# The carry of a chunked state-space scan: one 256-column product from high and low parts in place of two 128-column products

## The chip, the cores and the metric

The kernel runs on one core of one Trainium2 chip. A core has five engines that run side by side, each through its own list in order, and wait for one another by semaphores: TensorE (PE, matrix products), VectorE (DVE), ScalarE (ACT), GpSimd (POOL) and SyncE (SP, which here issues every DMA). The metric is the device time of one execution in microseconds (us), the median of several.

## The reference, cut to what matters

```python
x = x + mamba(layernorm(x), ...)      # 2 sequences x 512 tokens x 512 features, 128 heads of 64 columns, 8 groups
x = x + dense(layernorm(x)) + lora    # at the end, small

# inside mamba, per head (B and C are shared by the 16 heads of a group), 4 chunks of 128 tokens:
A_cum  = cumsum(A_dt, axis=-1)                                   # within each chunk
Y_diag = einsum('bzlhn,bzshn,bhzls,bzshp->bzlhp', Cc, Bc, L, xch)  # inside a chunk
states = einsum('bzlhn,bhzl,bzlhp->bzhpn', Bc, exp(A_cum[..., -1:] - A_cum), xch)
prev   = einsum('bhzc,bchpn->bzhpn', decay_chunk, states_p)[:, :-1]  # the state that enters each chunk
Y_off  = einsum('bzlhn,bzhpn,bhzl->bzlhp', Cc, prev, exp(A_cum))   # the carry: what it adds to the chunk
y = (Y_diag + Y_off + hs * D) * silu(gate)     # then a norm per group and an output product
```

The carry is `Y_off`: chunk 0 has none, chunks 1, 2 and 3 get the state that entered them, times their C, times a growth `exp(A_cum)`.

## The kernel before, in words

The work is cut into 64 **units** of two heads (128 feature columns) with both sequences (`b` = 0 and 1) in each. Eight units in a row make a **group**, which has one B and one C. I number the units 0 to 63; `k` is that number and `j` the place in the group, 0 to 7. Every engine has a loop over the groups with a body over `j`, written out by hand, and no scheduler moves anything. Projections and the output product are made with float32r operands (`F32R`), a number being cut into a high and a low part and three products summed (high by high, high by low, low by high). ACT makes each high part by a copy, POOL or DVE each low part by a subtraction.

In unit `k` the engines do this, in this order:

- **PE**: two output products of the pair before (`later_outs`), the projection of `x` for the next unit, `states` (L828 to L836, which waits for POOL's `xdecay`), `diagonal` (L838 to L846, which waits for DVE's `scores` and for two of DVE's output sums), the projection of the next gate, `carry` (L849 to L857, which waits for DVE's `state`), and two more output products. In units 4 and 5 of a group the next group's B and C are projected too.
- **DVE**: `scores`, then `xdt` (`to_heads`, L1357, from `quads`, which come by DMA), output sums, `y_low`, in units 1 to 3 of a group three or fewer normed sums, the three taps of the convolution of the next unit, `carried_state` (L1296), the block transpose of the next unit (`turn_blocks`, L1342), `skip`, `carry_part` (L1309) and `add_carry` (L1321) of both sequences, two output sums.
- **ACT**: the high part and the square of the unit before, `tap0` of the next (L1094, which waits for the projection of `x`), two weight high parts (L1072), then the decay factors, the SiLUs and the exponentials.
- **POOL**: `xdecay` (L1550, L1553), a weight low part (L1529), the running sum of squares (L1537), the low part of the output weight (L1571), a second weight low part, and the gate product of both sequences (`gated`, L1543).
- **SP**: in this order, among others, a weight load that waits for POOL's second low part (L702), the store of the turned blocks (`store_blocks`, L724, which waits for DVE's `turn_blocks`), the load of `quads` (L730, when the store has landed), and the growth rows of the next unit (`load_grown`, L717).

So SP's store stands behind its weight load: the blocks go out when DVE has turned them **and** POOL has made its second low part.

The carry before. `states` gives `P` columns for the carry of chunk 1 and, in the columns from `LATER * P`, the state at the middle, that is, the state which enters chunk 2. DVE copies it twice: as it is, and times the decay of chunk 2 (`chunk_tab`, a small table that has its own DMAs). `carry` then makes three float32 products of 128 columns per sequence: copy 0 by C of chunk 2, what chunk 2 itself adds (`xdecay[:, b, 2]`) by `bc_across[:, b, 1]`, and copy 1 by C of chunk 3, the last two summed. DVE multiplies the 384 columns by the growth rows and adds them to `y`.

## Time and profile before

| | |
|---|---|
| three runs | 1586.59, 1589.17, 1592.49 us; median 1589.17 |
| the profiled execution | 1586.06 us, of which its span is 1584.3 us |
| granted TensorE clock | 0.995 of full speed |
| busy, share of the span | PE 98%, PEld 82%, DVE 80%, ACT 72%, POOL 50% |
| DMA | 225.24 MB, 142 GB/s in the mean |

A row of a timeline has the start in us from the span's start, the time from the first start to the last end, the engine, the line, what is written and read, and how many in a row; brackets at its end give the time that the engine had been idle and who ended that. An engine pipelines: the next instruction can start a little before the row above has ended. PE's records are pipelined still more, so that a product's price is the distance from its start to the next start, not its length. A float32 product of 128 columns leaves two records, a float32r product one.

### The profile page before, as it was taken

How to read it: one execution, taken by the hardware profiler on the slowest of the kernel's cores; microseconds unless marked ns; L12 is line 12 of the kernel's file. 1: busy time of each engine (PE TensorE's matmuls, PEld its weight loads, DVE VectorE, ACT ScalarE, POOL GpSimd, SP SyncE). 2: the span in 40 equal slices, each digit the busy share in tenths (PEclk: the TensorE clock that was granted, in tenths of full speed). 3: DMA queues.
4: the chain of work that ended last, by engine and by line, in shares of the span. 5: the costliest groups of instructions: out<-in, count | busy, mean ns of one | idle time of the engine just before them, and what ended most of it. 6: DMA issues, size and time to landing. Idle time of an engine off the chain costs nothing.

```text
span 1584.3 us, 25865 instructions
## 1 busy us (share of the span) xinstructions
PE 1545.5 (98%) x9144; PEld 1304.9 (82%) x9144; DVE 1272.5 (80%) x1532; ACT 1142.7 (72%) x2020; POOL 790.6 (50%) x599
## 2 busy tenths in 40 slices
PE   7989999999999999999999999999999999999988
PEld 5768888888888888888888888878888888888877
DVE  6677777887879787887778878898778977798767
ACT  5976768875777667777687767767678767777743
POOL 2154545554545555455455545556544654555540
PEclk9999999999999999999999999999999999999999
DMA  4534445444444444543444444444444435444411
GB/s 153 203 113 152 130 144 168 155 135 146 139 148 152 148 140 128 170 160 115 159 156 151 134 154 146 137 147 156 130 147 165 150 120 165 142 150 150 131 44 53
DMA packets 130112, 225.24 MB, mean 142 GB/s; under 512 B 27840, under 2 KB 74944, under 8 KB 129728
## 3 DMA queue, kind: packets, MB, share of 16 engines
q1 hardware_dynamic: 129984, 223.59, 44.1%
q8 instruction: 73, 1.20, 0.3%
q14 instruction: 55, 0.45, 0.1%
HBM read 186.30 MB, written 37.23 MB: 141 GB/s over the span
## 4 chain that ended last, share of the span: by engine, by line
PE 44%; POOL 17%; DMA 13%; issue 11%; DVE 9%; ACT 4%; SPq 3%; DVEq 0%; POOLq 0%; ACTq 0%
DMA blocks_dram<-quads 7%; DMA quads<-blocks_dram 5%; POOL xdecay L1553 5%; POOL w_low L1529 4%; PE g_bank L824 4%; POOL square_sum L1537 4%; PE g_bank L826 4%; PE g_bank L825 4%; PE d_bank L845 4%; PE x_bank L826 3%; PE x_bank L824 3%; PE x_bank L825 3%; DVE xdt L1357 3%; SPq L730 2%; POOL out_low L1571 2%
## 5 line engine op out<-in xcount | busy, mean ns | idle before, releaser
L1082 ACT ACTIVATE scores<-scores,tables 128x128 f32<-128x128 f32 x1024 | 311.9, 389 | 0.0
L1543 POOL TENSOR_TENSOR y<-y,gate 128x512 f32<-128x512 f32 x128 | 190.1, 1506 | 209.3 <-DVE y L1325 209.3
L1529 POOL TENSOR_TENSOR w_low<-raw,w_high 128x512 fp32r<-128x512 f32 x139 | 186.1, 1339 | 202.5 <-ACT w_high L1072 202.5
L1261 DVE SCALAR_TENSOR_TENSOR hs<-x_bank,cols,hs 128x1022 f32<-128x1022 f32 x189 | 241.6, 1278 | 49.7 <-ACT hs L1094 45.1
L824 PE MATMUL g_bank<-x_high,w_high 128*128 128x512 f32 x624 | 250.5, 401 | 0.0
L826 PE MATMUL g_bank<-x_high,w_low 128*128 128x512 f32 x624 | 243.3, 390 | 0.0
L825 PE MATMUL g_bank<-x_low,w_high 128*128 128x512 f32 x624 | 243.2, 390 | 0.0
L1094 ACT ACTIVATE hs<-x_bank,cols 128x1024 f32<-128x1024 f32 x63 | 75.8, 1203 | 229.5 <-PE x_bank L826 167.8
L1293 DVE TENSOR_TENSOR scores<-scores,bc 128x1024 f32<-128x1024 f32 x128 | 188.3, 1510 | 16.4 <-ACT scores L1087 16.4
L824 PE MATMUL x_bank<-x_high,w_high 128*128 128x512 f32 x504 | 196.6, 390 | 0.0
L826 PE MATMUL x_bank<-x_high,w_low 128*128 128x512 f32 x504 | 196.1, 389 | 0.0
L825 PE MATMUL x_bank<-x_low,w_high 128*128 128x512 f32 x504 | 196.1, 389 | 0.0
L1550 POOL TENSOR_TENSOR xdecay<-xdt,tables 128x256 f32<-128x256 f32 x64 | 41.9, 655 | 306.3 <-DVE xdt L1357 292.1
L1357 DVE TENSOR_TENSOR xdt<-quads,tables 128x512 f32<-128x512 f32 x120 | 77.5, 687 | 89.2 <-DMA quads<-blocks_dram 85.8
L824 PEld LDWEIGHTS g_bank<-x_high,w_high 128*128 128x128 f32 x624 | 117.0, 188 | 33.2 <-issue 10.8
L1553 POOL TENSOR_TENSOR xdecay<-xdt,tables 128x384 f32<-128x384 f32 x128 | 143.4, 1141 | 0.0
L1537 POOL TENSOR_TENSOR square_sum<-square_sum,gate 128x1024 f32<-128x1024 f32 x55 | 139.1, 2530 | 0.0
L826 PEld LDWEIGHTS g_bank<-x_high,w_low 128*128 128x128 f32 x624 | 117.1, 188 | 25.4
L825 PEld LDWEIGHTS g_bank<-x_low,w_high 128*128 128x128 f32 x624 | 117.2, 188 | 22.4
L845 PE MATMUL d_bank<-scores,xdt 128*64 128x128 f32 x2048 | 126.6, 276 | 3.1 <-DVE acc L1380 2.2
L1087 ACT ACTIVATE scores<-scores 128x1024 f32<-128x1024 f32 x128 | 128.6, 1052 | 0.7
L845 PEld LDWEIGHTS d_bank<-scores,xdt 128*64 128x64 f32 x2048 | 111.0, 137 | 11.7 <-DVE acc L1380 3.4
(227 smaller groups left out, 3573.4 us busy)
## 6 DMA issues: line engine op xcount, KB each, us to landing
scores<-sums_dram SPq DMA_DIRECT2D x128, 512.0 KB, 5.0
raw<-w_in SPq DMA_DIRECT2D x144, 256.0 KB, 2.8
blocks_dram<-quads SPq DMA_DIRECT2D x60, 512.0 KB, 3.7
quads<-blocks_dram SPq DMA_DIRECT2D x240, 128.0 KB, 2.9
grown_rows<-grown_dram SPq DMA_DIRECT2D x256, 96.0 KB, 2.8
out_raw<-w_out SPq DMA_DIRECT2D x64, 256.0 KB, 3.0
mixed<-x SPq DMA_DIRECT2D x8, 256.0 KB, 4.9
out<-mixed SPq DMA_DIRECT2D x8, 256.0 KB, 2.0
```

The costliest lines, as they stand in the source:

```text
L824: pe.matmul(to, w_high[:, slot, k], x_high[:, b, k], start=(k == 0), stop=False)
L825: pe.matmul(to, w_high[:, slot, k], x_low[:, b, k], start=False, stop=False)
L826: mm = pe.matmul(to, w_low[:, slot, k], x_high[:, b, k], start=False, stop=(k == KT - 1))
L845: mm = pe.matmul(d_bank[r * HEAD_DIM:(r + 1) * HEAD_DIM, b, c * P:(c + 1) * P], xdt[:, b, c, r], scores[:, s, b, r, c], start=True, stop=True)
L1082: op = s.activation(at, at, ACT.Relu, bias=col[:, r, c:c + 1], scale=-1.0)
L1087: s.activation(scores[:, q % 2, b], scores[:, q % 2, b], ACT.Exp, scale=-1.0).then_inc(exp_ready, 1)
L1261: v.scalar_tensor_tensor(out=hs[:, q % 2, :, i:], in0=x_bank[:, :, 0:SEQ - i], scalar=cols[:, q, TAPS - 1 - i:TAPS - i], in1=hs[:, q % 2, ...
L1293: v.tensor_tensor(at, at, bc[:, b].rearrange("p c l -> p (c l)").unsqueeze(1) .to_broadcast([P, PAIR, SEQ]), ALU.mult).then_inc(scores_rea ...
L1529: pool.tensor_tensor(w_low[:, slot], raw[:, slot], w_high[:, slot].bitcast(F32), ALU.subtract)\
L1537: pool.tensor_tensor(square_sum[:], square_sum[:], gate[:, q % 2], ALU.add).then_inc(square_added, 1)
L1543: pool.tensor_tensor(y[:, b], y[:, b], gate[:, q % 2, b], ALU.mult).then_inc(y_ready, 1)
L1553: pool.tensor_tensor(xdecay[:, b, 0:LATER], xdt[:, b, 0:LATER], col.unsqueeze(3).to_broadcast([P, LATER, PAIR, HEAD_DIM]), ALU.mult)\
```

## The change

Chunks 2 and 3 lie side by side, so the state at the middle is multiplied by C of both at once, 256 columns, as three float32r products; what chunk 2 itself adds to chunk 3 becomes a product of its own into the first 128 columns. For this, the growth of chunk 3 is counted from the middle (the rows of chunk 3 get the sum at the end of chunk 2 as a bias), and chunk 3's own growth, for the separate product, takes the place of chunk 0's, which nobody used. In the loops:

- PE: `carry` is three float32r products of 256 columns and one float32 product of 128 columns for each sequence, in place of three float32 products of 128. It waits for `c_low_ready` in unit 0 of a group.
- DVE: `carried_state` writes a high part and then, after it, a low part, in place of two independent copies. `carry_part` covers 512 columns in place of 384.
- POOL: `gated` first adds 128 columns (the separate product) to chunk 3 of `y`, waits for that, and then multiplies by the gate. In unit 0 of each group POOL also makes `c_low`, 128x512, between its first weight low part and the sum of squares.
- SP: `load_grown` loads 512 columns a row in place of 384 and waits for POOL's new sum (`last_added`) in place of DVE's `y_sum`. The table `chunk_dram`, its stores, its loads and their waits are gone.
- ACT, before the loops: three exponentials for the growth (128, 256 and 128 columns) in place of one of 512; the copy for the chunk table is gone. `keep_c` writes a float32r tile of the same size.

```diff
@@ sync, prologue
-                sp.wait_ge(chunk_ready, b + 1)
-                sp.dma_start(chunk_by_head[b], chunk_decay[:, b]).then_inc(chunks_stored[b], 16)
...
@@ growth (ACT, prologue)
-                s.activation(grown[:, b], sums[:, b], ACT.Exp).then_inc(grown_ready, 1)
+                last = slice(LATER * P, (LATER + 1) * P)
+                s.activation(grown[:, b, 0:P], sums[:, b, last], ACT.Exp)
+                s.activation(grown[:, b, P:LATER * P], sums[:, b, P:LATER * P], ACT.Exp)
+                s.activation(grown[:, b, last], sums[:, b, last], ACT.Exp, bias=sums[:, b, last.start - 1:last.start])\
+                 .then_inc(grown_ready, 1)
...
-                s.activation(chunk_decay[:, b], grown[:, b, P - 1::P], ACT.Copy).then_inc(chunk_ready, 1)
@@ load_grown (SP)
-                reached(sp, y_sum, BATCH * (k - 1) + b + 1)
+                reached(sp, last_added, BATCH * (k - 1) + b + 1)
...
-                                 rows[r, P:].partition_broadcast(HEAD_DIM)).then_inc(grown_in[b], 16)
+                                 rows[r].partition_broadcast(HEAD_DIM)).then_inc(grown_in[b], 16)
@@ load_tables (SP)
-                reached(sp, state_ready, used)
-                load_chunks(g, b, half)
@@ states (PE)
-                pe.matmul(to[:, LATER * P:], b_tok[:, b, 0], part[:, 3], start=True, stop=False)
-                pe.matmul(to[:, LATER * P:], b_tok[:, b, 1], part[:, 1], start=False, stop=True)
-                pe.matmul(to[:, 0:P], part[:, 0], bc_across[:, b, 0], start=True, stop=True).then_inc(states_added, 1)
+                pe.matmul(to[:, 0:P], b_tok[:, b, 0], part[:, 3], start=True, stop=False)
+                pe.matmul(to[:, 0:P], b_tok[:, b, 1], part[:, 1], start=False, stop=True)
+                pe.matmul(to[:, P:2 * P], part[:, 0], bc_across[:, b, 0], start=True, stop=True).then_inc(states_added, 1)
@@ carry (PE)
-                pe.matmul(to[:, P:2 * P], state[:, b, 0].rearrange("p r d -> p (r d)"), c_feat[:, b, 0:P],
-                          start=True, stop=True)
-                pe.matmul(to[:, 2 * P:3 * P], xdecay[:, b, 2].rearrange("p r d -> p (r d)"), bc_across[:, b, 1],
-                          start=True, stop=False)
-                pe.matmul(to[:, 2 * P:3 * P], state[:, b, 1].rearrange("p r d -> p (r d)"), c_feat[:, b, P:],
-                          start=False, stop=True).then_inc(carried, 1)
+                pe.matmul(to[:, 2 * P:], state_high[:, b], c_high[:, b], start=True, stop=False)
+                pe.matmul(to[:, 2 * P:], state_high[:, b], c_low[:, b], start=False, stop=False)
+                pe.matmul(to[:, 2 * P:], state_low[:, b], c_high[:, b], start=False, stop=True)
+                pe.matmul(to[:, 0:P], xdecay[:, b, 2].rearrange("p r d -> p (r d)"), bc_across[:, b, 1],
+                          start=True, stop=True).then_inc(carried, 1)
@@ carried_state (DVE)
-                v.tensor_copy(state[:, :, 0], added_up).then_inc(state_ready, 1)
-                lost = chunk_tab[:, :, PAIR * q:PAIR * (q + 1), 2]
-                v.tensor_tensor(state[:, :, 1], added_up, lost.unsqueeze(3).to_broadcast([P, BATCH, PAIR, HEAD_DIM]),
-                                ALU.mult).then_inc(state_ready, 1)
+                v.tensor_copy(state_high[:], added_up).then_inc(state_ready, 1)
+                v.wait_ge(state_ready, 2 * k + 1)
+                v.tensor_tensor(state_low[:], added_up, state_high[:].bitcast(F32), ALU.subtract)\
+                 .then_inc(state_ready, 1)
@@ carry_part, add_carry (DVE)
-                v.tensor_tensor(rows, head_bank[b][:, 0:LATER * P], rows, ALU.mult).then_inc(carry_scaled, 1)
+                v.tensor_tensor(rows, head_bank[b], rows, ALU.mult).then_inc(carry_scaled, 1)
...
-                v.tensor_tensor(y[:, b, P:], y[:, b, P:], grown[:, b].rearrange("p c l -> p (c l)"), ALU.add)\
+                v.tensor_tensor(y[:, b, P:], y[:, b, P:], grown[:, b, 1:].rearrange("p c l -> p (c l)"), ALU.add)\
@@ gated (POOL)
                 pool.wait_ge(y_sum, u + 1)
+                pool.tensor_tensor(y[:, b, LATER * P:], y[:, b, LATER * P:], grown[:, b, 0], ALU.add)\
+                    .then_inc(last_added, 1)
+                pool.wait_ge(last_added, u + 1)
@@ body (POOL)
+                    if j == 0:
+                        pool.wait_ge(c_ready, g + 1)
+                        pool.tensor_tensor(c_low[:], bc_conv[:, 1, :, 2 * P:], c_high[:].bitcast(F32), ALU.subtract)\
+                            .then_inc(c_low_ready, 1)
```

On PE the place is the carry of one unit, between the gate projection and the output products; `c_feat`, `c_high` and `c_low` are C, `state*` the state at the middle, `group_parts` B and C put together. Before:

```order
L852 MATMUL head_bank<-c_feat,state 128x128
L854 MATMUL head_bank<-group_parts,xdecay 128x128
L856 MATMUL head_bank<-c_feat,state 128x128
L852 MATMUL head_bank<-c_feat,state 128x128
L854 MATMUL head_bank<-group_parts,xdecay 128x128
L856 MATMUL head_bank<-c_feat,state 128x128
```

Of the changed kernel, the same place:

```order
L839 MATMUL head_bank<-c_high,state_high 128x256
L840 MATMUL head_bank<-c_low,state_high 128x256
L841 MATMUL head_bank<-c_high,state_low 128x256
L842 MATMUL head_bank<-group_parts,xdecay 128x128
L839 MATMUL head_bank<-c_high,state_high 128x256
L840 MATMUL head_bank<-c_low,state_high 128x256
L841 MATMUL head_bank<-c_high,state_low 128x256
L842 MATMUL head_bank<-group_parts,xdecay 128x128
```

Six float32 products became six float32r products of twice the columns and two float32 ones; nothing else moved on PE.

On POOL the place is unit 0 of a group, from `xdecay` to the gate products. Before:

```order
L1553 TENSOR_TENSOR xdecay<-xdt,tables 128x384 x2
L1529 TENSOR_TENSOR w_low<-raw,w_high 128x512
L1537 TENSOR_TENSOR square_sum<-square_sum,gate 128x1024
L1571 TENSOR_TENSOR out_low<-out_raw,out_high 128x512
L1529 TENSOR_TENSOR w_low<-raw,w_high 128x512
L1543 TENSOR_TENSOR y<-y,gate 128x512 x2
```

Of the changed kernel, the same place:

```order
L1541 TENSOR_TENSOR xdecay<-xdt,tables 128x384 x2
L1514 TENSOR_TENSOR w_low<-raw,w_high 128x512
L1558 TENSOR_TENSOR c_low<-bc_conv,c_high 128x512
L1522 TENSOR_TENSOR square_sum<-square_sum,gate 128x1024
L1563 TENSOR_TENSOR out_low<-out_raw,out_high 128x512
L1514 TENSOR_TENSOR w_low<-raw,w_high 128x512
L1527 TENSOR_TENSOR y<-y,grown_rows 128x128
L1531 TENSOR_TENSOR y<-y,gate 128x512
L1527 TENSOR_TENSOR y<-y,grown_rows 128x128
L1531 TENSOR_TENSOR y<-y,gate 128x512
```

`c_low` now stands ahead of the second weight low part, in unit 0 of each group alone; the two sums of 128 columns stand ahead of the gate products in every unit.

## Rows read from the trace of the kernel before

**Rows 1.** The page: each engine's busy time, its share of the span, its instructions.

```profile
PE 1545.5 (98%) x9144; PEld 1304.9 (82%) x9144; DVE 1272.5 (80%) x1532; ACT 1142.7 (72%) x2020; POOL 790.6 (50%) x599
```

**Rows 2.** Waits: engine, line, for whom; us in total, times, longest.

```profile
PE head_bank L834 <- POOL xdecay L1553: 12.7, 8, 3.3
```

**Rows 3.** Timeline of PE in unit 32, from the gate projection into the carry.

```profile
823.25 0.39 PE L826 MATMUL g_bank<-x_high,w_low 128*128 128x512 f32 x1
823.48 0.38 PE L852 MATMUL head_bank<-c_feat,state 128*128 128x128 f32 x2
823.70 0.39 PE L854 MATMUL head_bank<-group_parts,xdecay 128*128 128x128 f32 x2
```

**Rows 4.** Timelines of POOL, DVE and SP in unit 32, by start.

```profile
816.58 1.29 POOL L1529 TENSOR_TENSOR w_low<-raw,w_high 128x512 fp32r<-128x512 f32 x1 [2.43 <-ACT w_high L1072]
821.44 1.30 POOL L1529 TENSOR_TENSOR w_low<-raw,w_high 128x512 fp32r<-128x512 f32 x1
821.77 1.25 DVE L1342 STREAM_TRANSPOSE quads<-hs 128x1024 f32<-128x1024 f32 x1 [1.18 <-ACT hs L1106]
822.77 0.33 SPq L702 DMA_DIRECT2D raw<-w_in  x1
823.27 0.32 SPq L724 DMA_DIRECT2D blocks_dram<-quads  x1
831.53 1.29 DVE L1357 TENSOR_TENSOR xdt<-quads,tables 128x512 f32<-128x512 f32 x2 [0.39 <-DMA quads<-blocks_dram]
```

**Rows 5.** Timelines of DVE and SP in units 33 and 35, by start.

```profile
843.81 1.25 DVE L1342 STREAM_TRANSPOSE quads<-hs 128x1024 f32<-128x1024 f32 x1 [0.77 <-ACT hs L1106]
845.09 0.32 SPq L724 DMA_DIRECT2D blocks_dram<-quads  x1
...
886.21 1.25 DVE L1342 STREAM_TRANSPOSE quads<-hs 128x1024 f32<-128x1024 f32 x1 [0.46 <-ACT hs L1106]
887.82 0.32 SPq L724 DMA_DIRECT2D blocks_dram<-quads  x1
```

**Rows 6.** Timelines of POOL and PE: `xdecay` and `states` of units 33 and 36.

```profile
833.48 2.63 POOL L1553 TENSOR_TENSOR xdecay<-xdt,tables 128x384 f32<-128x384 f32 x2
837.29 0.39 PE L834 MATMUL head_bank<-xdecay,group_parts 128*128 128x128 f32 x2
...
898.28 2.62 POOL L1553 TENSOR_TENSOR xdecay<-xdt,tables 128x384 f32<-128x384 f32 x2
900.95 0.49 PE L834 MATMUL head_bank<-xdecay,group_parts 128*128 128x128 f32 x2
```

**Rows 7.** Timelines of DVE and PE: output sums and `diagonal` of unit 38.

```profile
954.48 1.28 DVE L1380 TENSOR_TENSOR acc<-d_bank,acc 128x512 f32<-128x512 f32 x2
955.21 1.86 PE L845 MATMUL d_bank<-scores,xdt 128*64 128x128 f32 x30 [0.17 <-DVE acc L1380]
```

**Rows 8.** Groups of DVE by line and shape: busy us, mean ns, idle before.

```profile
L1313 DVE TENSOR_TENSOR grown_rows<-head_bank,grown_rows 128x384 f32<-128x384 f32 x128 | 70.1, 555 | 23.7 <-PE head_bank L856 16.6
L1380 DVE TENSOR_TENSOR acc<-x_bank,acc 128x512 f32<-128x512 f32 x96 | 64.9, 686 | 19.7 <-PE x_bank L894 19.5
```

**Rows 9.** Timelines of ACT and POOL behind the gate products of unit 35.

```profile
893.27 1.16 ACT L1130 ACTIVATE y_high<-y,cols 128x1024 fp32r<-128x1024 f32 x1 [0.47 <-POOL y L1543]
897.70 0.62 POOL L1550 TENSOR_TENSOR xdecay<-xdt,tables 128x256 f32<-128x256 f32 x1 [4.46 <-DVE xdt L1357]
900.24 1.21 ACT L1094 ACTIVATE hs<-x_bank,cols 128x1024 f32<-128x1024 f32 x1 [4.34 <-PE x_bank L826]
```

**Rows 10.** Timeline of DVE: `scores` of units 35 and 39.

```profile
871.54 2.78 DVE L1293 TENSOR_TENSOR scores<-scores,bc 128x1024 f32<-128x1024 f32 x2
969.47 2.36 DVE L1293 TENSOR_TENSOR scores<-scores,bc 128x1024 f32<-128x1024 f32 x2 [1.14 <-ACT scores L1087]
```

**Rows 11.** Timeline of ACT at the start: exponentials of the prologue, and the end of unit 0.

```profile
40.60 0.97 ACT L434 ACTIVATE one_plus<-head_sums 128x128 f32<-128x128 f32 x3
...
85.15 1.16 ACT L1130 ACTIVATE y_high<-y,cols 128x1024 fp32r<-128x1024 f32 x1 [1.97 <-POOL y L1543]
```

56 lines of the change are left out of this document (22 added, 34 removed).

## The prediction

> **What bounds the kernel now.** I read the page first: PE is busy for 98% of the span, DVE for 80, ACT for 72, POOL for 50 [rows 1]. So a saving on PE should count, if PE is never kept waiting. Then the waits: PE waited for POOL's `xdecay` 12.7 us in all, in 8 waits over the threshold of the view [rows 2]. That is little, but it shows a second path almost as long as PE's. I followed it through one group, units 32 to 39, on the timelines of all engines.
>
> It starts when the projection of `x` ends. ACT makes `tap0` and two weight high parts, POOL the first weight low part at 816.58 and the second from 821.44 to 822.74; SP's weight load has waited for this, goes at 822.77, and the store of the blocks behind it at 823.27. DVE had turned the blocks at 821.77 + 1.25 = 823.02 [rows 4]. So in unit 32 POOL is last by a quarter of a microsecond. `xdt` of unit 33 starts at 831.53, that is 8.26 us after the store. In unit 33 DVE is last (turned at 845.06, stored at 845.09), in unit 35 POOL's side again (886.21 + 1.25 = 887.46, stored at 887.82, 0.36 later) [rows 5]; unit 34 looks like unit 32, POOL last by 0.25.
>
> How long this path is against PE's is seen at `states`. In unit 33 the second sequence's `xdecay` is ready at 836.11 and PE takes it at 837.29: 1.18 us to spare. In unit 36 it is ready at 900.90 and PE takes it at 900.95: PE waits [rows 6]. The spare time melts by about 0.4 us a unit from unit 1 to unit 4 of a group, since DVE's normed sums make its round longer than PE's; units 5 and 6, in which PE projects B and C too, bring it back. The seven whole groups after the first all look like this: in unit 4 PE takes the second `xdecay` as it comes (within 0.06 us).
>
> There is a second such place: in unit 38 `diagonal` starts at 955.21, as DVE's first output sum from 954.48 ends (half of 1.28 us) [rows 7]. That sum stands behind a chain that hangs on the `x` projection of unit 37, and it does not move when PE's carry gets shorter.
>
> **What PE saves.** A float32r product of 512 columns takes 823.48 - 823.25 = 0.23 us, a float32 product of 128 columns 823.70 - 823.48 = 0.22 us in two records, 0.11 each [rows 3]. No product of 256 float32r columns is in the trace. Its bounds are one record of 0.11 below and the 512-column product of 0.23 above; I take 0.116, near the lower, since half of 0.23 is that. Carry before: 6 x 0.223 = 1.34 us a unit. Carry after: 6 x 0.116 + 2 x 0.223 = 1.14 us. PE saves **0.20 us a unit**, 12.8 us over 64 units if every unit gave its own. With 0.11 it is 0.23 a unit; with 0.23 the carry gets 0.49 us longer. The Trainium skill ("TensorE: Matmul & The Clock Gate", section "Back-to-back issue gap") gives N/2.4 + 2.5 ns, which is 0.109 us for 256 columns; for 512 it gives 0.216, where this trace has 0.23. By the page a unit would save 0.24.
>
> **What of it counts.** Per group of eight carries. The carries of units 0 to 3 only bring PE sooner to a wait in unit 4, on a path that starts at the beginning of unit 0. The carry of unit 5 only brings it sooner to the wait in unit 6 [rows 7]. Left are the carries of units 4, 6 and 7: -0.60 us a group. Had the other path stayed as it is but for its own POOL and SP parts, which start from PE's projections and move up with them, unit 4 would give back up to another 0.6.
>
> **c_low.** A POOL subtraction of 128x512, priced like the weight low part, 1.29 us [rows 4] (1.27 from start to start where two follow each other). It stands in unit 0 ahead of the second weight low part, and POOL is already last there: SP's load goes 1.27 us later, the store with it, and `xdt` of unit 33 too. Unit 33's 1.18 us of spare time are gone, and DVE's path carries the delay on: the turn of unit 33, where DVE is last, moves by the full 1.27. In units 34 and 35, where POOL's side was last by 0.25 and 0.36 us and hangs on PE's projections, DVE's delay must first eat those: 1.27 - 0.25 - 0.36 = 0.66 us are left at unit 36, where nothing was to spare. So a group costs **+0.66** and gains 0.60: **+0.06 us**, +0.4 for seven groups. Group 0 has no stored blocks in its first units: -0.60. The last group has no wait in unit 6 (it projects no B and C): -0.20.
>
> **The other edits.** DVE's `carry_part` grows from 384 to 512 columns, from 555 ns to about 686, the time of the 512-column sum that also reads PSUM [rows 8]: 0.26 us a unit. DVE then waits for PE's second output product (19.7 us in all in [rows 8]) and again for `quads` (0.39 in [rows 4]), so nothing is added while that cover lasts; without it, 0.26 us a unit in three or four units a group. `carried_state`'s low part now follows its high part: some 0.1 us inside the wait for ACT's SiLU, 0.46 to 1.18 us [rows 4, 5]: nothing. POOL's two sums of 128 columns: half of 128x256, 0.31 us [rows 9], plus a wait for itself, say 0.42 each, 0.85 a unit. Behind them POOL waits 4.46 us for `xdt`; ACT, whose high part waits for them, later waits 4.34 us for PE [rows 9]: nothing in the loops. SP's `load_grown` waits for POOL's sum, which is done before SP has issued the `quads`; queued behind it is only the next output weight. The growth rows are a third larger; they are issued right behind the `quads` and could slow their last piece: 0 to 0.1 us at some four stores a group, I take +0.8 us for the kernel. The chunk table's DMAs, of a few bytes, were on no path that ends last: nothing.
>
> **Start.** The growth's exponentials: three of about 0.32 us [rows 11] for one of twice that, on ACT, which feeds the first table: +0.4. At the end of unit 0 ACT waits 1.97 us for POOL's gate product [rows 11] and the next `tap0` follows: POOL's sums cost their 0.8 there. Together +1.2.
>
> **Sum.** +0.4 - 0.60 - 0.20 + 0.8 + 1.2 = **+1.6 us**. The profiled execution took 1586.06 us, so it would take 1587.6. It lies 3.1 below the median of the three, 1589.17; on the median I put 1590.8.
>
> **Rivals.** *(a) The gain comes through.* `c_low` falls into a hole after all, or POOL's and SP's side moves up with PE as reckoned above. For it: DVE's turn and POOL's part are within 0.4 us of each other, and a small shift decides who is last. Against: at unit 32 POOL's chain from 816.58 on has no hole before SP's load. Then a group gives 0.60 + 0.60 = 1.2: -8.4 - 0.6 - 0.2 + 0.8 + 1.2 = -7.2, **1582.0** on the median; with 0.11 for a product and no waits at all 1576.
>
> *(b) POOL and DVE get in each other's way: slower.* DVE's `scores` took 2.36 us without POOL beside them and 2.78 with its gate product [rows 10]. POOL's gate products now end 0.85 us later, deeper into `scores`, and DVE comes 0.26 later on its own. It decides when both together exceed the cover in front of `xdt`, 0.39 us in unit 32 plus what `c_low` adds there. Price: 0.42 + 0.26 - 0.39 = 0.3 us at four units of eight groups, 9.3, with a sum of +1.6 in front: +11, **1600**. The Trainium skill ("SBUF — State Buffer", section "Who interferes with whom") says that a DVE instruction with two SBUF inputs and a GpSimd one that reads SBUF exclude each other, the later blocked until the first is done, and that is the rule which speaks most against this change: every new POOL sum starts as DVE adds the other sequence's carry from two SBUF inputs. By that rule [rows 10] agree.
>
> *(c) The 256-column product costs 0.23*, as a 512-column one does: the carry grows by 0.49 us a unit, on PE, which has no cover: +31 us, **1621**. Nothing speaks for it but that the trace does not show the form.
>
> *(d) It does not do what it says*, that is, PE's carry is not shorter, 0.15 us or more for a product: the sum is then near +4, inside the forecast.
>
> **How the numbers follow.** A difference of 0.5% (8 us) is about what a measurement of this kernel can tell from none. Forecast, with (d): 0.58, at 1590.8, its own range 1586 to 1596. (a) 0.23, of which about two thirds lie over 0.5% faster. (b) 0.16, nearly all over 0.5% slower. (c) 0.03. Faster 0.17, same 0.65, slower 0.18. The range takes in (a) at its reckoned size with some of its better end, and (b) at its price: 1578 to 1600.
>
> **What would show it.** PE's carry in unit 32: distances of about 0.116 us between the 256-column records; 0.11 or 0.23 decide (a)'s end or (c). POOL's `c_low` between the first weight low part and the squares, and SP's store of unit 32 about 1.3 us further from that low part than 6.7 us; if it is not, `c_low` was hidden. The waits of PE for `xdecay`: they should grow from 12.7 us to 20 or more, in units 1 to 4, by about what PE saves there. PE's busy time should fall by some 12 us while the span stays. DVE's `scores`: if their mean rises by 0.2 us or more and DVE no longer waits for `quads`, it is (b). A span that is 7 us or more shorter would prove the walk through the group wrong at its step from unit 33 to unit 36; one that is 8 us longer would mean that a cover called sufficient above was not.

## The result and the profile after

The changed kernel took 1621.6 us in the median of four runs (1617.9 to 1624.5), the kernel before 1587.9 in the same session: 1.0205 times as long, with an interval of 1.0181 to 1.0229. The forecast was 1590.8 and its range ended at 1600. The profiled execution of the changed kernel took 1620.7 us with a span of 1619.0, 34.7 more than the span of the kernel before. One execution of `c_low_short` below (2567 us) and one of `before_squares_last` (7057 us), with a granted clock of 0.56 and 0.21 where all others had 0.94 or more, are in no median, ratio or interval here.

The page of the changed kernel, which answers to [rows 1], with the first two lines on the chain that ended last:

```profile
PE 1548.3 (96%) x9016; PEld 1294.3 (80%) x9016; DVE 1352.8 (84%) x1532; ACT 1143.2 (71%) x2022; POOL 944.9 (58%) x735
...
DVE 24%; DMA 20%; POOL 18%; issue 13%; PE 12%; ACT 8%; SPq 5%; DVEq 0%; POOLq 0%; ACTq 0%
DMA blocks_dram<-quads 10%; DMA quads<-blocks_dram 9%; POOL w_low L1514 5%; DVE xdt L1342 4%; DVE hs L1249 4%; DVE mixed L1369 4%; POOL xdecay L1541 4%; POOL square_sum L1522 4%; SPq L728 4%; DVE y_low L1265 2%; POOL out_low L1563 2%; ACT scores L1068 2%; DVE scores L1281 2%; DVE acc L1365 2%; ACT hs L1094 1%
```

PE's own share of the chain is 12%: the end is now set by a ring of DVE, the two transfers of the blocks, and POOL. DVE is busy for 80 us more than in [rows 1] and POOL for 154 more, though DVE was given only 12 us of new work (`carry_part`) and POOL some 64 by the forecast's prices (128 sums of 0.42, eight `c_low` of 1.3). Of DVE's 80 us, the normed sums took 31, `scores` 24, `xdt` 13 and `carry_part` 12. What goes beyond the new work is time in which one was held up by the other. The waits say where it comes out, as in [rows 2] (engine, line, for whom; us in total, times, longest):

```profile
ACT y_high L1118 <- POOL y L1531: 125.6, 49, 6.0
PE head_bank L821 <- POOL xdecay L1541: 34.3, 45, 3.5
PE head_bank L839 <- DVE state_low L1290: 11.4, 10, 1.1
```

PE's wait for `xdecay` went from 12.7 us in 8 waits to 34.3 in 45, and its wait for the state ahead of the carry from 1.0 us to 11.4. These 32 us are nearly all of the 34.7. ACT's wait for the gated `y` was 24.6 us in 32 waits before.

Measured from the start of one unit's `states` to the next, the loss is very uneven. It sits mainly in units 2 and 3 of the groups, which took 21.1 to 21.5 us in the kernel before (but for one at 23.5 and one at 22.1) and now take either 22.0 to 22.1 or 24.2 to 24.3. Of the fourteen such units in the seven groups behind the first, ten are of the second kind and four of the first. The seven units 3 lost 20.3 us together, the units 2 9.8, the units 4 4.5 and the units 1 3.6. Group 0, which has no normed sums, took 190.7 us in both kernels. PE's ten waits for the state stand in just the ten units of 24.2 to 24.3 us, 1.12 to 1.15 us in each. The split of the state is at most some 0.1 us of each: the kernel before has one such wait too, of 1.02 us, in its one unit of 23.5 us. Units 0, 5 and 7 are 0.14 us shorter than before wherever PE does not wait in them.

In the kernel before, in unit 35 (unit 3 of its group, `states` at 878.90), DVE and POOL read:

```profile
878.61 2.65 DVE L1384 SCALAR_TENSOR_TENSOR mixed<-acc,g_rstd,mixed 128x512 f32<-128x512 f32 x3
881.18 2.59 DVE L1261 SCALAR_TENSOR_TENSOR hs<-x_bank,cols,hs 128x1022 f32<-128x1022 f32 x2
...
880.94 1.45 POOL L1529 TENSOR_TENSOR w_low<-raw,w_high 128x512 fp32r<-128x512 f32 x1 [1.55 <-ACT w_high L1072]
882.37 2.40 POOL L1537 TENSOR_TENSOR square_sum<-square_sum,gate 128x1024 f32<-128x1024 f32 x1
```

and in the changed kernel (`states` at 895.78):

```profile
892.68 1.55 DVE L1342 TENSOR_TENSOR xdt<-quads,tables 128x512 f32<-128x512 f32 x2 [0.76 <-DMA quads<-blocks_dram]
...
896.73 5.80 DVE L1369 SCALAR_TENSOR_TENSOR mixed<-acc,g_rstd,mixed 128x512 f32<-128x512 f32 x3
902.46 3.90 DVE L1249 SCALAR_TENSOR_TENSOR hs<-x_bank,cols,hs 128x1022 f32<-128x1022 f32 x3
...
897.47 1.72 POOL L1514 TENSOR_TENSOR w_low<-raw,w_high 128x512 fp32r<-128x512 f32 x1
899.15 2.83 POOL L1522 TENSOR_TENSOR square_sum<-square_sum,gate 128x1024 f32<-128x1024 f32 x1
901.94 1.74 POOL L1563 TENSOR_TENSOR out_low<-out_raw,out_high 128x512 fp32r<-128x512 f32 x1
911.63 0.71 POOL L1527 TENSOR_TENSOR y<-y,grown_rows 128x128 f32<-128x128 f32 x1 [6.69 <-DVE y L1310]
912.42 1.29 POOL L1531 TENSOR_TENSOR y<-y,gate 128x512 f32<-128x512 f32 x1
913.68 1.44 POOL L1527 TENSOR_TENSOR y<-y,grown_rows 128x128 f32<-128x128 f32 x1
915.20 2.15 POOL L1531 TENSOR_TENSOR y<-y,gate 128x512 f32<-128x512 f32 x1
...
917.38 1.16 ACT L1118 ACTIVATE y_high<-y,cols 128x1024 fp32r<-128x1024 f32 x1 [3.31 <-POOL y L1531]
919.91 1.19 ACT L1080 ACTIVATE hs<-x_bank,cols 128x1024 f32<-128x1024 f32 x1
```

DVE's three normed sums (`mixed += acc * g_rstd`) took 2.65 us and the taps began 2.28 behind `states`. Now the sums begin 1.2 us later against `states`, take 5.80, and the taps begin 6.68 behind `states`. 1.2 us of lateness have become 4.4. The turn, the store and all that follows move with it. Lower down, POOL's two sums and two gate products take 5.7 us where the two gate products took 2.80, ACT waits 3.31 us for them, and the next `tap0` starts at 919.91 without any wait for PE, where it waited 4.34 in [rows 9].

### The profile page after: what moved, and what is told of

It reads as the page before. It is cut to its first block, busy times and chain, and to the rows that moved or that the text cites. A ratio compares the mean times of both kernels' runs of the same rounds, so it can differ in the third digit from the quotient of the medians.

```text
span 1619.0 us, 25697 instructions
## 1 busy us (share of the span) xinstructions
PE 1548.3 (96%) x9016; PEld 1294.3 (80%) x9016; DVE 1352.8 (84%) x1532; ACT 1143.2 (71%) x2022; POOL 944.9 (58%) x735
## 4 chain that ended last, share of the span: by engine, by line
DVE 24%; DMA 20%; POOL 18%; issue 13%; PE 12%; ACT 8%; SPq 5%; DVEq 0%; POOLq 0%; ACTq 0%
DMA blocks_dram<-quads 10%; DMA quads<-blocks_dram 9%; POOL w_low L1514 5%; DVE xdt L1342 4%; DVE hs L1249 4%; DVE mixed L1369 4%; POOL xdecay L1541 4%; POOL square_sum L1522 4%; SPq L728 4%; DVE y_low L1265 2%; POOL out_low L1563 2%; ACT scores L1068 2%; DVE scores L1281 2%; DVE acc L1365 2%; ACT hs L1094 1%
## 5 line engine op out<-in xcount | busy, mean ns | idle before, releaser
L1527 POOL TENSOR_TENSOR y<-y,grown_rows 128x128 f32<-128x128 f32 x128 | 109.3, 854 | 236.9 <-DVE y L1310 236.9
L1531 POOL TENSOR_TENSOR y<-y,gate 128x512 f32<-128x512 f32 x128 | 220.6, 1724 | 10.0
L1281 DVE TENSOR_TENSOR scores<-scores,bc 128x1024 f32<-128x1024 f32 x128 | 211.8, 1693 | 14.1 <-ACT scores L1073 14.1
L1118 ACT ACTIVATE y_high<-y,cols 128x1024 fp32r<-128x1024 f32 x63 | 72.5, 1151 | 125.6 <-POOL y L1531 125.6
L1342 DVE TENSOR_TENSOR xdt<-quads,tables 128x512 f32<-128x512 f32 x120 | 90.6, 795 | 84.2 <-DMA quads<-blocks_dram 81.5
L1522 POOL TENSOR_TENSOR square_sum<-square_sum,gate 128x1024 f32<-128x1024 f32 x55 | 143.1, 2602 | 0.0
```

What stands on the lines that cost most here:

```text
L1281: v.tensor_tensor(at, at, bc[:, b].rearrange("p c l -> p (c l)").unsqueeze(1) .to_broadcast([P, PAIR, SEQ]), ALU.mult).then_inc(scores_rea ...
L1342: v.tensor_tensor(xdt[:, :, :, r], quads[:, r * PER_HEAD:(r + 1) * PER_HEAD].rearrange("p h b c i -> p (b c) h i"), col.unsqueeze(3).to_br ...
L1522: pool.tensor_tensor(square_sum[:], square_sum[:], gate[:, q % 2], ALU.add).then_inc(square_added, 1)
L1531: pool.tensor_tensor(y[:, b], y[:, b], gate[:, q % 2, b], ALU.mult).then_inc(y_ready, 1)
```

## The experiments

Two theories stood at the start. *Theory S*: POOL's two sums of 128 columns, between DVE's `add_carry` and the gate product, are the cause, since they push the gate products deep into DVE's `scores`. *Rival C*: it is `c_low`, 1.3 us in unit 0 of each group. From the fifth run on there was *theory N* (a step at the normed sums) against *rival L* (a sum of added work). Each ratio is against runs of the kernel before on the same chip; where a text speaks of so many us over the kernel before, it is the difference of the two medians in this table. A trace is of one execution, and not always of a typical one: those of `before_pool_fill` (1598.2 us), `squares_last` (1608.7), `before_late_14` (1602.2) and `normed_later` (1617.9) took 6 to 9 us more than the median of their kernel, that of `no_sum` (1592.9) took 15 less.

| kernel | median us | kernel before | ratio (interval) |
|---|---|---|---|
| changed kernel | 1621.6 | 1587.9 | 1.0205 (1.0181 to 1.0229) |
| sum_on_dve | 1614.1 | 1587.3 | 1.0165 (1.0134 to 1.0197) |
| c_low_short | 1615.2 | 1587.3 | 1.0183 (1.0151 to 1.0216) |
| before_pool_sums | 1593.1 | 1587.3 | 1.0040 (1.0014 to 1.0067) |
| before_pool_fill | 1592.5 | 1587.3 | 1.0027 (1.0010 to 1.0044) |
| normed_short | 1599.9 | 1586.8 | 1.0091 (1.0072 to 1.0110) |
| before_normed_short | 1587.6 | 1586.8 | 1.0010 (0.9998 to 1.0022) |
| squares_last | 1600.7 | 1586.8 | 1.0106 (1.0078 to 1.0133) |
| no_sum | 1608.1 | 1586.6 | 1.0138 (1.0102 to 1.0174) |
| before_late_07 | 1589.2 | 1586.6 | 1.0016 (0.9997 to 1.0036) |
| before_late_14 | 1592.7 | 1586.6 | 1.0060 (1.0029 to 1.0091) |
| sum_early_sq | 1589.7 | 1586.6 | 1.0022 (1.0002 to 1.0043) |
| normed_later | 1611.1 | 1588.7 | 1.0146 (1.0125 to 1.0168) |
| before_normed_later | 1589.5 | 1588.7 | 1.0014 (0.9996 to 1.0031) |
| all_three | 1598.6 | 1588.7 | 1.0061 (1.0049 to 1.0074) |
| no_sum_c_short | 1594.6 | 1588.7 | 1.0039 (1.0017 to 1.0061) |
| sum_early | 1613.3 | 1585.2 | 1.0176 (1.0149 to 1.0203) |
| before_squares_last | 1583.4 | 1586.8 | 0.9985 (0.9972 to 0.9998) |
| before_squares_last_2 | 1584.8 | 1585.2 | 0.9989 (0.9974 to 1.0004) |

**One piece at a time.** `sum_on_dve` takes the sums from POOL:

```diff
-                pool.tensor_tensor(y[:, b, LATER * P:], y[:, b, LATER * P:], grown[:, b, 0], ALU.add)
...
+            def add_last(k, b):      # on DVE, ahead of its add_carry
+                v.tensor_tensor(grown[:, b, LATER], grown[:, b, LATER], grown[:, b, 0], ALU.add)
```

> The changed kernel, but DVE adds the extra term of chunk 3 (grown slot 0 into grown slot 3, 128 columns for each sequence) ahead of its own sum, and POOL adds nothing. All else of the change stays, c_low on POOL too. Theory S (POOL's sums, which stand between DVE's sum and the gate product, are what costs the 34 us): the time falls to 1586 to 1596, ACT's wait for POOL's y goes back from 125.6 us to below 50, the fourth unit of a group from 24.2 to about 21.2 us. Rival C (it is c_low, 1.3 us in unit 0 of each group, that tips the group into the slow round): 1615 to 1625, since DVE even gets 0.4 us a unit more to do.

`c_low_short` cuts `c_low` to 8 columns after group 0:

```diff
+                        cut = slice(0, 8) if g > 0 else slice(0, 2 * P)
...
-                        pool.tensor_tensor(c_low[:], bc_conv[:, 1, :, 2 * P:], c_high[:].bitcast(F32), ALU.subtract)
+                        pool.tensor_tensor(c_low[:, :, cut], bc_conv[:, 1, :, 2 * P:][:, :, cut], c_high[:, :, cut]..., ALU.subtract)
```

> The changed kernel, but after group 0 POOL computes only 8 of the 256 columns of c_low for each sequence, so that the carries use a stale low part; the instruction, its waits and its place stay, its 1.3 us go. Theory S: the time stays slow, 1612 to 1619 (the forecast's own price of c_low, 0.66 us a group, is 4.6 in all; up to 9 with 1.3 a group). Rival C: 1583 to 1592.

`before_pool_sums` puts only a sum ahead of the gate product of the kernel before, `before_pool_fill` a fill in its place. In both, SP's growth load waits for the new instruction too:

```diff
                 pool.wait_ge(y_sum, u + 1)
+                pool.tensor_tensor(grown[:, b, 2], y[:, b, LATER * P:], grown[:, b, 2], ALU.add).then_inc(last_added, 1)
+                pool.wait_ge(last_added, u + 1)
```

> The kernel before, with only one thing of the change: a POOL sum of 128 columns ahead of each gate product, with the wait of the gate product for it and of SP's growth load for it. It reads y and the used growth rows and writes into the latter, so the result is the same; DVE, PE and c_low are as before. Theory S: this alone brings the slow round: 1610 to 1625, ACT's wait for y above 90 us, the fourth unit near 24 us. Rival C, and the forecast's own reckoning (0.85 us a unit, covered): 1588 to 1592.

> The kernel before, with a POOL instruction at the same place that reads no SBUF: it fills the used growth rows (384 columns) with a constant. Two forms of theory S: if the cost is that a POOL sum with two SBUF inputs and a DVE one shut each other out, a fill is not held up, takes below 0.5 us, and the time stays within 1587 to 1597. If the cost is only that the gate product starts later and lands deeper in DVE's scores, the fill costs as much as the sum did for each 0.1 us that it takes: 1605 or more when it takes 0.4 us or more. Rival C: 1588 to 1592.

Neither theory stood. Without POOL's sums 1614, without `c_low` 1615, and with the sums alone 1593. The first value is weak against S, since DVE paid for its two sums (321 ns each in the mean, 36 us in all); the third is not. C said 1583 to 1592 where 1615 came. Nor had either removal cleared the units 2 and 3: in the traces, eight of fourteen were still at 24.2 to 24.4 us in `c_low_short` and six at 24.0 in `sum_on_dve`, with ten in the changed kernel.

The fill is worth a look. POOL's groups in `before_pool_fill`, and DVE's `scores` of that kernel:

```profile
L1543 POOL MEMSET grown_rows<- 128x384 f32 x128 | 53.6, 418 | 217.8 <-DVE y L1326 217.8
...
L1294 DVE TENSOR_TENSOR scores<-scores,bc 128x1024 f32<-128x1024 f32 x128 | 222.0, 1773 | 15.8 <-ACT scores L1088 15.7
```

The fill was never held up (418 ns in the mean, 0.42 in each row looked at), where the sum took 784, and yet it cost about as much, +5 against +6. What it did was to start the gate products 0.5 us later, and DVE's `scores` rose from 1510 ns in the mean to 1773. So the new instruction's own collision hardly matters, and the likely cost is the gate product behind it, which lands in `scores`; that the later growth load, which both versions share, costs nothing was not tested. This is rival (b) of the prediction. In the trace of `before_pool_sums` all fourteen units 2 and 3 are at 21.4 to 21.9 us: there it is seen by itself, and is worth some 6 us. The trace of `before_pool_fill` has four of them at 23.6 to 23.7, so part of its loss, and of the 1773, is already what the next runs are about. The time, 1592.5, lies in the range of the first form of S (1587 to 1597) and far under the 1605 of the second, whose mechanism the rows show: it is real, and small.

The Trainium skill ("SBUF — State Buffer", section "Who interferes with whom") says that a DVE instruction with two SBUF inputs contends with a GpSimd instruction that reads SBUF, and not with one that only writes it. The fill at 0.42 us beside the sum at 0.78 agrees.

**The normed sums.** `normed_short` and `before_normed_short` cut them to 8 of 512 columns:

```diff
+                cut = slice(0, HID if done == GROUPS else 8)
-                v.scalar_tensor_tensor(out=mixed[:, at], in0=acc[:, at], ...
+                v.scalar_tensor_tensor(out=mixed[:, at, cut], in0=acc[:, at, cut], ...
```

> The changed kernel, but DVE's normed sums (mixed += acc * g_rstd, three in unit 2 and 3 of a group, two in unit 1) work on 8 of 512 columns for groups 0 to 6, so that most of those groups' share of the output is left out. The instructions, their waits and their places stay. Neither the POOL sums alone (1593 us) nor c_low (1617 without it) explained the loss. New theory N: the pieces of the change make DVE about 1.3 us later in units 2 and 3, and that is a step, not a slope: the second and third normed sum then run beside POOL's weight low part and squares and take 1.76 and 2.87 us instead of 0.74 each. Without their length there is nothing to collide: 1572 to 1582, no unit 3 of 24.2 us, and 0 to 9 us faster than the kernel before with the same cut. Rival L (the loss is the sum of the work added to a round of DVE and DMA that is simply too long, and the sums are only the last of many): still 15 us or more slower than the kernel before with the same cut.

> The kernel before with the same cut: normed sums on 8 of 512 columns for groups 0 to 6, most of their share of the output left out. Both theories: 0.7 us less in units 2 and 3 for each normed sum while DVE's round binds, so PE's wait for xdecay goes from 12.7 us to near 5: 1576 to 1586. It is here as the partner of the changed kernel with this cut.

The kernel before gained nothing from the cut, so there the sums are covered. Of the changed kernel's 34 us over the kernel before, 12 remain between the two with the cut. N said 0 to 9 us faster, L 15 or more slower, and the truth lies between. Unit 3 is back at 21.3 us in six of seven groups. In the seventh, group 3, even sums of 8 columns met POOL: the second and third took 1.30 and 2.41 us, where they take 0.21 elsewhere, and units 2 and 3 took 22.8 us each. So a sum with next to no work of its own is held up much as a full one is, and the cut did not take the collision away everywhere. What stays is unit 2, at 21.8 to 22.2 in all groups but one, where the gate products hold up the second `scores`.

**Lateness in doses.** In `before_late_07` and `before_late_14` DVE makes one or two of its output sums twice in unit 3:

```diff
+                    if g > 0 and j == 2 and c in (2, 3):      # (3,) in before_late_07
+                        v.tensor_copy(to, bank_of(j, c)).then_inc(again, 1)
+                        v.wait_ge(again, 2 * (g - 1) + (2, 3).index(c) + 1)
+                        v.tensor_tensor(to, bank_of(j, c), to, ALU.max).then_inc(added, 1)
...
```

> The kernel before, with DVE made late on purpose at one place: in unit 3 of groups 1 to 7, one of the output sums ahead of y_low is made twice (a second instruction of 0.69 us that reads PSUM and writes the same values, with a wait of some 0.06). Result unchanged. Theory N: of the three normed sums only the last meets the weight low part (it should take 1.7 instead of 0.74): the taps of unit 3 start 1.7 us later; the time 1589 to 1596. Rival L (a slope of one): 0.75 x 7 = 5 us at most, 1587 to 1592. The two overlap here; the next run tells.

> The same with two such instructions, 1.5 us in unit 3 of groups 1 to 7. Theory N: the second normed sum waits for the weight low part and the third for the squares (1.76 and 2.87 us, as in the changed kernel), the taps start 4.4 us later, unit 3 goes from 21.1 to near 24 us: 2.5 to 3 us in 7 groups, 1604 to 1611. Rival L: 1.5 x 7 = 10 us at most, and less as there is cover: 1590 to 1597.

The medians lie nearer to L than to N: `before_late_14` came into L's range, 11 us under N's. But the traces show the step itself, in kernels with nothing of the change in them. Three units 3, DVE's normed sums: of `before_late_14` at unit 35, where two doses were given (`states` at 880.30); of `before_late_07` at unit 35, with one dose, where the blocks had also come late (`states` at 881.36); and of `before_late_14` at unit 43 (`states` at 1069.22):

```profile
881.21 3.09 DVE L1389 SCALAR_TENSOR_TENSOR mixed<-acc,g_rstd,mixed 128x512 f32<-128x512 f32 x3
```

```profile
878.14 1.29 DVE L1358 TENSOR_TENSOR xdt<-quads,tables 128x512 f32<-128x512 f32 x2 [1.36 <-DMA quads<-blocks_dram]
882.74 5.31 DVE L1389 SCALAR_TENSOR_TENSOR mixed<-acc,g_rstd,mixed 128x512 f32<-128x512 f32 x3
883.41 1.28 POOL L1534 TENSOR_TENSOR w_low<-raw,w_high 128x512 fp32r<-128x512 f32 x1 [1.68 <-ACT w_high L1073]
884.66 2.84 POOL L1542 TENSOR_TENSOR square_sum<-square_sum,gate 128x1024 f32<-128x1024 f32 x1
```

```profile
1071.13 5.23 DVE L1389 SCALAR_TENSOR_TENSOR mixed<-acc,g_rstd,mixed 128x512 f32<-128x512 f32 x3
```

Sums that start 0.91 us behind `states` take 3.09, and unit 35 is as long as ever, 21.14 us. Sums that start at 1.38 take 5.31, and the unit takes 25.2. Half a microsecond makes 2.2. POOL's first weight low part starts 2.05 us behind `states` in these units (2.00 in units 2), since it hangs on PE, by way of ACT; in unit 35 of the changed kernel it is 1.69, as PE had itself waited 0.49 us just ahead of `states`. If the second normed sum has begun by then, only the third is hit; if not, the second waits for the weight low part and the third for the squares. So it is a step, as N says. The changed kernel shows it more narrowly still: in unit 10 the sums start 0.71 us behind `states` and take 3.67, in unit 11 they start at 0.87 and take 5.80, and the units take 21.98 and 24.20. The first sum has a length of its own: 1.32 us where POOL's last `xdecay` runs beside it, and 0.74 where not. So the 2.65 of the kernel before already hold one meeting; without any, three sums take 2.07.

What N had wrong is how often 1.5 us are enough to reach it. In five of seven groups two doses left unit 3 at 21.1 to 21.5 us (DVE's wait for `quads` shrinks instead). Units 43 and 51, the two that reached the step, stood behind a unit 2 that had reached it without any dose (23.67 us each), as unit 42 of the kernel before does by itself (5.81 us for the sums, 23.52 for the unit). So these runs show the height of the step, and not that 1.5 us of lateness reach it. Four of fourteen units 2 and 3 were at the step in the profiled execution of 1602.2 us, while five of the nine executions took 1591 to 1593.

**What makes DVE late enough.** `no_sum` drops POOL's sums, `no_sum_c_short` drops them and cuts `c_low`:

> The changed kernel without POOL's two sums a unit and with nothing in their place, so that one term of chunk 3 is left out of the output; c_low, DVE's wider carry_part and PE's product stay. Theory N, refined by the last runs (POOL's gate products hold up DVE's second scores, DVE comes later, and in unit 3 the late normed sums run into POOL's weight low part and squares, which makes 4 us of 1.3): without the sums the lateness in unit 3 is that of c_low and carry_part, 0.3 to 0.9 us, at most one normed sum is hit: 1583 to 1592. That would be, with the 6 us of the POOL sums alone, far less than the 34 us of both together: a step. Rival L (costs add up): POOL sums alone gave 6, so the rest of the change must cost 28 by itself: 1610 to 1616.

> The changed kernel without POOL's sums (one term of chunk 3 left out) and, after group 0, with c_low cut to 8 of 256 columns. What is left of the change in the loops is PE's product, DVE's carry_part of 512 columns and the split of the state. Without the sums alone it took 1592.9 to 1612.8 in four executions, 1608 in the median. Theory N: c_low made DVE late from unit 1 on, carry_part alone (0.26 us a unit) reaches the second step only: 1580 to 1592, with at most 3 of 14 units 2 and 3 above 23 us. Rival W (the wider carry_part and the split state are the main cost): 1600 to 1610, as without the sums alone.

`no_sum` gave 1592.9, 1605.0, 1611.2 and 1612.8 us: now here, now there, as a kernel at the edge of a step would, and outside both ranges in the median. Only the fastest of the four has a trace, with three units 2 and 3 above 23 us; that the slower ones have more was not seen. With `c_low` cut as well it is 1594.6; W falls by the median, though four of its ten executions took 1599 to 1603, and N's upper end is missed by 2.6. Put together, in us over the kernel before:

| | `c_low` whole | `c_low` cut |
|---|---|---|
| POOL's sums | +34 | +28 |
| no sums | +22 | +6 |

The pieces do not add up. Either of the two, on top of the 6 of what is left (the longer `carry_part`, the split state, less PE's gain), is enough to bring back most of the loss (with the sums, the trace shows eight of fourteen units at the step; with `c_low`, it is the median that says so), and together they cost only 6 us more than the dearer one. That is why taking one piece away told so little.

**Moving work instead of removing it.** `squares_last` and `before_squares_last_2` move POOL's squares behind `out_low` and the second weight low part:

```diff
-                    if prev:
-                        add_squares(*prev)
                     pool.wait_ge(out_high_ready, k + 1)
...
                     for at in splits[1:2]:
                         low_part(*at)
+                    if prev:
+                        add_squares(*prev)
```

> The changed kernel, complete, with one instruction of POOL moved: the sum of squares (2.4 to 2.8 us) stands behind out_low and the second weight low part instead of ahead of them, in every unit. Theory N: DVE's late normed sums then meet a weight low part or out_low of 1.3 us where they met the squares of 2.8, SP's weight load and the store behind it are no longer held up by the squares, and the step is not reached in most groups: 1585 to 1600, fewer than half of the units 3 at 24 us. Rival L: POOL's order changes nothing in DVE's work: 1612 to 1622.

> The kernel before with POOL's squares behind the second weight low part, once more with more rounds, since the first measurement (ratio 0.9985, 0.9972 to 0.9998) had an unusable profile. Expected: again 1582 to 1586, ratio 0.997 to 1.000; in the profile a second weight low part that ends 2.4 us earlier in the units where it was last, and PE's wait for xdecay below 12.7 us. If it is 1.000 or above, the first was chance and no version here beats the kernel before.

In the changed kernel this leaves 14 us of the 34, but not for the reason expected: in the traced execution, 8 us over the median, eleven of fourteen units are still at the step. It is only lower. DVE's three sums in unit 35 of `squares_last`:

```profile
890.52 4.70 DVE L1369 SCALAR_TENSOR_TENSOR mixed<-acc,g_rstd,mixed 128x512 f32<-128x512 f32 x3
```

4.70 instead of 5.80, as the third sum waits for an `out_low` and not for the squares, and these units take 23.0 to 23.2 us instead of 24.3. In the kernel before the same move gave 0.9985 (0.9972 to 0.9998) and, measured again, 0.9989 (0.9974 to 1.0004): some 2 us if anything. It is the only version here that stands below the kernel before. The sign named for it, PE's wait for `xdecay` below 12.7 us, did not come: 14.6.

> The kernel before, complete, with the same move of POOL's squares behind the second weight low part. Theory N: here the normed sums end as the weight low part begins, so little changes; POOL's second weight low part comes 2.4 us earlier, which takes POOL off the path in units 32 and 34 of the walk: 1582 to 1588. Rival L: the same. A time above 1592 would say that the squares, now beside the taps and the SiLU, hold up something else.

`sum_early` makes POOL's sum right behind `carry_part`, ahead of `add_carry`; `sum_early_sq` does that and moves the squares:

```diff
+            def last_early(q, k, b):
+                pool.wait_ge(carry_scaled, u + 1)
+                pool.tensor_tensor(grown[:, b, LATER], grown[:, b, LATER], grown[:, b, 0], ALU.add).then_inc(last_added, 1)
...
-                v.wait_ge(carry_scaled, u + 1)      # in DVE's add_carry
+                v.wait_ge(last_added, u + 1)
```

> The changed kernel, complete, with only one of the two moves of the version at 1589.7 us: POOL's sum for chunk 3 stands right behind DVE's carry_part instead of ahead of the gate product; the squares stay where the change has them. If the place of the sum is what matters (it keeps DVE's scores from being met by two more POOL instructions and lets ACT have y in time): 1588 to 1597, most of the 32 us. If both moves are needed, as the squares alone gave back 21 us of the 34: 1600 to 1612.

> The changed kernel, complete, with two instructions of POOL in other places: squares behind the second weight low part, and the sum for chunk 3 (grown slot 0 into slot 3) right behind DVE's carry_part instead of between DVE's add_carry and the gate product; add_carry waits for it. Theory N: the gate products then start about 0.5 us later than before instead of 1.2 to 3.3, scores are hit as before, the normed sums too: 1582 to 1592, ACT's wait for POOL's y back below 50 us. Against: add_carry now waits for POOL, some 0.5 us a unit on DVE, whose round is the longest in units 1 to 3; if this is as late as the sum was, 1596 to 1602, as with the squares moved alone (1600.7).

The sum's place alone leaves 28 of the 34 us, the squares' place alone 14, both together 3: 1589.7 us. As with the removals, the parts do not tell the whole: alone they gave back 6 and 20 us, together 31. With both, the complete change came into N's range of 1582 to 1592, though N had expected the normed sums to be hit as before, and most were not. Unit 35 of `sum_early_sq` (`states` at 878.64), POOL, DVE and ACT:

```profile
889.16 1.37 POOL L1528 TENSOR_TENSOR grown_rows<-grown_rows 128x128 f32<-128x128 f32 x2 [2.06 <-DVE grown_rows L1298]
890.49 1.29 POOL L1535 TENSOR_TENSOR y<-y,gate 128x512 f32<-128x512 f32 x1
892.29 1.29 POOL L1535 TENSOR_TENSOR y<-y,gate 128x512 f32<-128x512 f32 x1 [0.50 <-DVE y L1310]
...
878.43 2.65 DVE L1369 SCALAR_TENSOR_TENSOR mixed<-acc,g_rstd,mixed 128x512 f32<-128x512 f32 x3
893.33 2.47 DVE L1281 TENSOR_TENSOR scores<-scores,bc 128x1024 f32<-128x1024 f32 x2
...
893.61 1.15 ACT L1118 ACTIVATE y_high<-y,cols 128x1024 fp32r<-128x1024 f32 x1 [1.00 <-POOL y L1535]
```

The gate products take 1.29 us each and are all but out of the way as `scores` begin, which take 2.47 for the two instead of 3.04. The normed sums are back at 2.65. Eleven of fourteen units 2 and 3 are at 21.1 to 21.9 us, three at 23.0 to 23.1.

`normed_later` and `before_normed_later` move the normed sums from ahead of the taps to behind the turn; `all_three` is `sum_early_sq` with that move:

```diff
-                    if g > 0:
-                        for at in {1: (0, 1), 2: (2, 3, 4), 3: (5, 6, 7)}.get(j, ()):
-                            normed_out(g, at)
...
                             turn_blocks(k + 1)
+                        if g > 0:
+                            for at in {1: (0, 1), 2: (2, 3, 4), 3: (5, 6, 7)}.get(j, ()):
+                                normed_out(g, at)
```

> The changed kernel, complete, with only DVE's normed sums of units 1 to 3 moved: from ahead of the taps to behind the turn of the blocks, where POOL has ended its squares and waits for y. Theory N (steps: where the second normed sum meets POOL's first weight low part, 2.05 us behind the states, the taps come 2.7 us later at once; ten of the fourteen units 2 and 3 of the changed kernel are there and have 24.2 to 24.3 us, the others 22.0): no unit of 24 us is left, the sums take 0.74 us each, 1585 to 1597. Rival L (DVE has too much to do in these units wherever the sums stand): 1605 or more.

> The kernel before with the same move. Theory N: the turn comes earlier against POOL, everything behind it 2.2 us later, the round no shorter: 1582 to 1592, and no unit of 23 us or more, of which the kernel before has one now and then. Rival L: the same.

> The changed kernel, complete, with the three moves together: squares behind the second weight low part, the sum for chunk 3 right behind carry_part, normed sums behind the turn. Theory N: DVE's round stays below PE's, which has 0.14 us a unit less to do: 1576 to 1586, the first version below the kernel before by more than 2 us. If it is 1586 to 1592, the moved sums only trade one wait for another, and PE's 9 us stay hidden behind DVE's round.

This is the sharpest test of N, and N does not come out whole. No normed sum is held up any more (739 ns in the mean), no unit 3 is above 21.9, and still 1611. Unit 18 of `normed_later` takes 23.9 us, and POOL, DVE, ACT and PE ahead of it and in it show another collision:

```profile
488.45 2.15 POOL L1531 TENSOR_TENSOR y<-y,gate 128x512 f32<-128x512 f32 x1
489.68 2.07 DVE L1342 TENSOR_TENSOR xdt<-quads,tables 128x512 f32<-128x512 f32 x2 [0.23 <-DMA quads<-blocks_dram]
490.63 1.15 ACT L1118 ACTIVATE y_high<-y,cols 128x1024 fp32r<-128x1024 f32 x1 [4.63 <-POOL y L1531]
493.30 0.49 PE L821 MATMUL head_bank<-xdecay,group_parts 128*128 128x128 f32 x2 [0.91 <-POOL xdecay L1541]
495.08 0.49 PE L821 MATMUL head_bank<-xdecay,group_parts 128*128 128x128 f32 x2 [0.84 <-POOL xdecay L1541]
```

The second gate product, at 488.45, ends so late that it blocks not only `scores` but `xdt` (2.07 us instead of 1.28), `xdecay` follows, and PE waits twice, 1.75 us. The kernel before gains nothing by the same move (1589.5 against 1588.7). So 11 of the 34 us went with the collision at the normed sums, 22 stayed, and what the trace shows for these is the late gate products. `all_three` was expected at 1576 to 1586 and gave 1598.6, 10 us over the kernel before where `sum_early_sq` has 3: the sums now stand in front of `carry_part`, and the gate products of units 2 and 3 start 13.0 to 13.7 us behind `states` where in `sum_early_sq` most start at 11.9 to 12.1.

## Why the prediction was wrong

**What bounds the kernel: right.** The second path, DVE's turn to `xdt` and `xdecay`, did decide, and PE's waits for `xdecay` grew beyond 20 us in units 1 to 4, as named. (PE projects B and C in units 4 and 5, not 5 and 6; nothing hangs on that.)

**PE's saving: right in kind.** The three products of 256 columns and the float32 ones behind them, PE in unit 36:

```profile
930.19 0.28 PE L839 MATMUL head_bank<-c_high,state_high 128*128 128x256 f32 x1
930.30 0.28 PE L840 MATMUL head_bank<-c_low,state_high 128*128 128x256 f32 x1
930.42 0.28 PE L841 MATMUL head_bank<-c_high,state_low 128*128 128x256 f32 x1
930.54 0.39 PE L842 MATMUL head_bank<-group_parts,xdecay 128*128 128x128 f32 x2
930.68 0.36 PE L839 MATMUL head_bank<-c_high,state_high 128*128 128x256 f32 x1
930.89 0.28 PE L840 MATMUL head_bank<-c_low,state_high 128*128 128x256 f32 x1
...
931.27 0.48 PE L878 MATMUL x_bank<-out_high,y_high 128*128 128x512 f32 x1
```

and in the kernel before the instruction behind the carry, which had begun at 823.48 [rows 3]:

```profile
824.74 0.48 PE L892 MATMUL x_bank<-out_high,y_high 128*128 128x512 f32 x1
```

The distances are 0.11 to 0.12, as taken, and rival (c) falls. One, from the first 256-column product behind a float32 one to the next (930.68 to 930.89), is 0.21. The whole carry takes 1.08 us, where it took 1.26 and not the 1.34 of the prediction. It is 0.18 shorter, and a unit without waits 0.14, where 0.20 was forecast; where the other 0.04 went was not found. That term was 0.06 too large, 3.8 us over 64 units, and it is not what went wrong. That the time measured, 1621.6, is rival (c)'s 1621 is chance, since its mechanism is absent. PE's busy time, which should have fallen by some 12 us, rose from 1545.5 to 1548.3: a record lasts longer than the distance to the next (0.28 against 0.11), so a wait adds to it. That sign was not fit for its purpose.

**`c_low`: right for one unit, wrong for what follows.** In unit 32 the store of the blocks stands 836.77 - 828.83 = 7.94 us behind the first weight low part, 1.25 more than in [rows 4] (forecast 1.27):

```profile
828.83 1.28 POOL L1514 TENSOR_TENSOR w_low<-raw,w_high 128x512 fp32r<-128x512 f32 x1 [1.97 <-ACT w_high L1058]
830.07 1.30 POOL L1558 TENSOR_TENSOR c_low<-bc_conv,c_high 128x512 fp32r<-128x512 f32 x1
836.77 0.32 SPq L722 DMA_DIRECT2D blocks_dram<-quads  x1
846.26 1.29 DVE L1342 TENSOR_TENSOR xdt<-quads,tables 128x512 f32<-128x512 f32 x2 [2.10 <-DMA quads<-blocks_dram]
```

`xdt` started 1.2 us later still, as SP's four issues for the `quads` took longer and their data came late. The step that failed is the next one, "DVE's delay must first eat those: 1.27 - 0.25 - 0.36 = 0.66 us are left at unit 36". A delay was carried through units 2 and 3 by subtraction. In these units a late DVE meets POOL where an early one doesn't: 1.2 us of lateness became 4.4 in unit 35, 2.1 of it at one stroke, where the second normed sum comes too late (3.67 us to 5.80 for the three). The prediction had the length of the normed sums in its argument ("make its round longer than PE's"), but took that length as fixed; it is 2.65 us in the trace before and 5.80 in the changed kernel.

**POOL's sums: wrong in both halves.** "Say 0.42 each, 0.85 a unit": they took 854 ns in the mean with the gate products 218 ns longer each, and the way from DVE's first `add_carry` to the gated y became 2.9 us longer in unit 35. "Nothing in the loops", since POOL has 4.46 us behind them and ACT 4.34: that cover was read for POOL and for ACT, but not for DVE, whose `scores` and `xdt` have little cover (0.39 us in [rows 4]) and stand in the gate products' way. Groups of DVE and POOL in the changed kernel:

```profile
L1281 DVE TENSOR_TENSOR scores<-scores,bc 128x1024 f32<-128x1024 f32 x128 | 211.8, 1693 | 14.1 <-ACT scores L1073 14.1
L1369 DVE SCALAR_TENSOR_TENSOR mixed<-acc,g_rstd,mixed 128x512 f32<-128x512 f32 x64 | 88.6, 1427 | 0.3
L1342 DVE TENSOR_TENSOR xdt<-quads,tables 128x512 f32<-128x512 f32 x120 | 90.6, 795 | 84.2 <-DMA quads<-blocks_dram 81.5
L1527 POOL TENSOR_TENSOR y<-y,grown_rows 128x128 f32<-128x128 f32 x128 | 109.3, 854 | 236.9 <-DVE y L1310 236.9
L1531 POOL TENSOR_TENSOR y<-y,gate 128x512 f32<-128x512 f32 x128 | 220.6, 1724 | 10.0
```

Before, `scores` took 1510 ns, the normed sums 936 and `xdt` 687.

**Rival (b) named the right mechanism, at a third of the price.** It had the pair of gate product and `scores`, said 1600, and got a chance of 0.16. Its own sign came true in part: `scores` rose by 0.18 us in the mean, close to the 0.2 named, but DVE still waited for `quads`, 81.5 us where it had been 85.8. What it left out is that POOL and DVE meet at three more places (normed sums with weight low part and squares, `xdt` with gate product, POOL's sum with `scores`), and that at one of them the loss is a step. By itself the mechanism as the rival put it is worth about the 6 us of `before_pool_sums`, less than the 11 forecast.

**`carry_part`, the start, the growth rows.** `carry_part` took 683 ns, as forecast (686). It is in the +6 of `no_sum_c_short` with the split state and PE's gain, and was not taken apart further. The start did not lose the 1.2 us forecast: at unit 1 the profiled execution was 1.9 us ahead. The chunk table's loads were of 16 KB each and not of a few bytes; no run shows that it mattered.

**What stays open.** Why PE's 0.14 us a unit, 9 us over the kernel, never comes through, not even in `sum_early_sq`, is seen only in part: in its trace nearly all units 0, 1, 5 and 7 have the gain, four of seven units 2 (21.1 to 21.2) do not, three units 3 at 23.0 to 23.1 take 6 us back, and group 0 is 2.5 us longer. The 6 us that are left without sums and `c_low` were not divided.

## What to carry to other kernels

An instruction that is added to an engine off the critical path is not covered by that engine's idle time alone: ask which instructions of the other engine it, and all behind it, will run beside, and whether those have cover. Where two engines shut each other out, a delay is not to be subtracted from spare time but followed to the next meeting, with the durations for both orders. When removing any one piece of a change barely helps, look for a step that each piece alone can reach, and move work away from the meeting point rather than take it out.

## What was not expected of the hardware

A POOL instruction that reads no SBUF was not held up at all beside DVE's two-input sums (418 ns in the mean over 128), while a sum of a third of its columns took 784 to 854 there.

A ring of two engines and two transfers settled into lengths with gaps between them, 21.1 to 21.5, about 22 and 24.2 to 24.3 us, and one kernel (`no_sum`) fell now nearer the one, now the other: 1592.9 to 1612.8 us in four executions, a spread of 20 us where 24 executions of the kernel before spread over 12.

A DVE sum of 8 columns, 0.21 us by itself, took 2.41 us beside POOL's sum of squares of 2.37 (`normed_short`, units 26 and 27): there it is POOL's instruction that sets the length, not the work of its own.
